# Layer 1 with two single tiles and seven pairs, and differences of weight blocks taken from PSUM while the weights are still being made

## The reference, cut to what matters

```
x: (32, 64, 1024) fp32; condition c[b] in 0..15; two layers, each  x = x + ffn(mix(x))
mix:    m[b] = W_cond[c[b]]^T x[b]           (a 64 x 64 matrix for each of the 32 samples)
layer 0 ffn:  m @ ternary(w0) * column scale + b0            (w0: 1024 x 1024)
layer 1 ffn:  m @ w^T + bias + 4 * (m @ A^T) @ B^T
        w = NF4_LEVELS[q_weight] * q_scale per group of 64   (1024 x 1024), A: 8 x 1024, B: 1024 x 8
```

## Time and profile before

| | us |
|---|---|
| median of 3 runs (lowest, highest) | 360.81 (360.71, 360.83) |
| profiled execution, device time | 360.83 |
| its span | 359.0 |
| TensorE busy | 352.2 (98%) |
| VectorE busy | 242.0 (67%) |
| ScalarE busy | 161.1 (45%) |
| GpSimd busy | 224.7 (63%) |

### The profile page before, as it was taken

One profiled execution on the slowest core, in us unless ns is written; L12 is line 12 of the kernel. 1 busy time (PEld: TensorE's weight loads), 2 busy tenths in 40 slices (PEclk: granted clock), 3 DMA queues, 4 the chain that ended last, 5 costly groups with the idle time before them and its releaser, 6 DMA issues.

```text
span 359.0 us, 5496 instructions
## 1 busy us (share of the span) xinstructions
PE 352.2 (98%) x1832; PEld 298.7 (83%) x1832; DVE 242.0 (67%) x363; ACT 161.1 (45%) x285; POOL 224.7 (63%) x146
## 2 busy tenths in 40 slices
PE   8899999999999999999999999999999999999996
PEld 8768788888888888888888888888888888888884
DVE  5789969896996899873899979355262452634523
ACT  2787467776886877752232314213041130321300
POOL 0488999986976888876520220866366663666632
PEclk9999999999999999999999999999999999999999
DMA  6894411953345245333311330304215032150202
GB/s 235 289 328 138 151 31 30 339 203 115 134 168 181 88 156 203 125 120 121 108 76 62 123 118 3 120 0 155 88 63 181 1 140 103 60 182 2 117 31 88
DMA packets 27838, 44.63 MB, mean 124 GB/s; under 512 B 8834, under 2 KB 17026, under 8 KB 27810
## 3 DMA queue, kind: packets, MB, share of 16 engines
q1 hardware_dynamic: 26242, 43.67, 35.0%
q10 hardware_dynamic: 1568, 0.61, 0.7%
HBM read 27.49 MB, written 16.78 MB: 123 GB/s over the span
## 4 chain that ended last, share of the span: by engine, by line
PE 87%; DVE 3%; POOL 2%; issue 2%; ACT 2%; SPq 1%; DMA 1%; POOLq 0%; DVEq 0%; ACTq 0%
PE acc L1157 33%; PE acc L1195 32%; PE xT L1121 10%; PE acc L1137 6%; PE spare L1121 3%; POOL col_scale L596 2%; PE acc L1222 2%; DMA w_in<-in_L_ffn_w 1%; PE acc L1224 1%; DVE hl L872 1%; PE xT L1204 1%; DVE W L925 1%; ACT hh L684 0%; SPq L428 0%; SPq L426 0%
## 5 line engine op out<-in xcount | busy, mean ns | idle before, releaser
L569 POOL TENSOR_TENSOR X<-X,bias 128x1024 f32<-128x1024 f32 x28 | 67.5, 2412 | 29.3 <-PE xT L1121 29.1
L1157 PE MATMUL acc<-T,hh 128*128 128x512 f32 x192 | 76.0, 396 | 0.0
L1157 PE MATMUL acc<-T,hl 128*128 128x512 f32 x192 | 75.0, 391 | 0.0
L723 ACT ACTIVATE spare<-q_raw 128x512 f32<-128x512 int32 x96 | 56.0, 598 | 19.1 <-DVE side_p L913 5.1
L1195 PE MATMUL acc<-W,hh 128*128 128x512 f32 x192 | 61.1, 389 | 0.0
L1021 DVE TENSOR_TENSOR X<-X,acc 128x512 f32<-128x512 f32 x36 | 24.8, 688 | 34.8 <-PE acc L1195 18.6
L1121 PEld LDWEIGHTS xT<-mix,X 128*128 128x128 f32 x352 | 42.7, 192 | 1.5
L1121 PE MATMUL xT<-mix,X 128*128 128x128 f32 x352 | 42.8, 275 | 0.0
L1195 PEld LDWEIGHTS acc<-W,hh 128*128 128x128 f32 x192 | 36.0, 188 | 7.5
L1157 PEld LDWEIGHTS acc<-T,hl 128*128 128x128 f32 x192 | 36.1, 188 | 7.4
L628 POOL TENSOR_TENSOR X<-X,ys 128x512 f32<-128x512 f32 x18 | 22.6, 1286 | 31.1 <-DVE ys L1010 31.1
(11 more groups left out here) (98 smaller groups left out, 662.0 us busy)
## 6 DMA issues: line engine op xcount, KB each, us to landing
out<-X SPq DMA_DIRECT2D x26, 512.0 KB, 3.0
X<-out SPq DMA_DIRECT2D x16, 512.0 KB, 3.4
X<-in_x SPq DMA_DIRECT2D x12, 512.0 KB, 3.4
q_raw<-in_L_ffn_q_weight SPq DMA_DIRECT2D x16, 256.0 KB, 3.0
w_in<-in_L_ffn_w SPq DMA_DIRECT2D x14, 256.0 KB, 6.5
x_first<-in_x SPq DMA_DIRECT2D x4, 512.0 KB, 4.6
out<-x_first SPq DMA_DIRECT2D x4, 512.0 KB, 6.8
out<-X SPq DMA_DIRECT2D x4, 256.0 KB, 2.0
```

What stands on the lines that cost most here:

```text
L569: pool.tensor_tensor(x_of(g), x_of(g), (bias1 if g >= NT else bias)[:, :], ALU.add).then_inc(s_xb, 1)
L723: act.activation(dst, q_raw[:, d % QS, :, :].rearrange("p o i -> p (o i)"), ACT.Copy, scale=slope, bias=offset).then_inc(s_line, 1)
L1157: mm = pe.matmul(acc[:, bank_of(q), :], a[:, k, :], b, start=(k == 0 and j == 0), stop=(k == KB - 1 and j == len(terms) - 1))
```

## The change

Layer 1 gets two single tiles and seven pairs (`SB = NT + 2`). T1 and T3 are now made during layer 0. ScalarE copies the transposed pieces r = 0 and 1 out of PSUM unrounded (`keep_block`), into the place where the low part of T2 and T3 will be. When the next piece (r = 1 or 2) lies in PSUM, VectorE subtracts the kept one from it (`sum_T13`), ScalarE rounds the difference (`high_T13`) and VectorE writes its low part over it (`low_T13`). T2 and T4 are made in the two single tiles: 24 instructions of VectorE and 8 of ScalarE, dealt out by `SUMS_BY`. `turn_w` of a piece r = 2 or 3 waits for `sum_T13` too. `lines_by` places on ScalarE each line that a maximum of an earlier half tile needs ahead of that half tile's end. The weights lie in SBUF in a new order, so the wait for the spilled first tiles moves from T1's high part to `high_w(4)`. Where low parts were read from, their plain form has the same address (`W01_sums`, `W23_sums`, `W_T4_sums`).

```diff
     WARM = 10
-    SB = NT + 4
...
 
-    W_ORDER = (T1, T2, B11, B21, B22, T3, B12)
-
-
-    NTS = 12
-    COMPLETE = ((T1, 3), (T3, 5), (T2, 6), (T4, 10))
+    W_ORDER = [(B11, 1), (B12, 1), (B21, 1), (B22, 1), (B11, 0), (B12, 0), (B21, 0), (B22, 0),
+               (T1, 0), (T1, 1), (T2, 0), (T2, 1), (T3, 0), (T3, 1)]
+
+
+    NTS = 6
+    SUMS_BY = (0, 8, 15, 21, NTS * HB + 1)
...
 
+    def lines_by(m):
+
+        done = share(2 * NC * ND, m)
+        if done == 0:
+            return 0
+        d, c = divmod(done - 1, 2 * NC)
+        sign, j = divmod(c, NC)
+        return max(share(2 * NL * ND, m), 2 * NL * d + NL * sign + j + 2)
+
     def sums_by(m):
 
-        return NTS * HB * (m - NH * NT) // (NH * (SB - NT))
+        return SUMS_BY[m - NH * NT]
...
 
             if c == T4:
                 return W_T4[:, part, j, :]
-            return (W01, W23)[j // 2][:, W_ORDER.index(c), part, j % 2, :]
...
-            return plain({T1: 1, T3: 3, T2: 4, T4: 5}[c])
+        def as_is(c, j):
+
+
+            if c == T4:
+                return W_T4_sums[:, 1, j, :]
+            return (W01_sums, W23_sums)[j // 2][:, W_ORDER.index((c, j % 2)), 1, :]
...
 
@@ -727,19 +754,33 @@
                 act.wait_ge(s_wT, d + 1)
                 if d == 0:
                     act.wait_ge(s_acc, NH * F)
+                if d == 4:
+                    for t in range(F):
+                        act.wait_ge(s_spill[t], 16)
...
-                            act.activation(w1(0, c, j), t_plain(c), ACT.Copy).then_inc(s_Th, 1)
+            def keep_block(d):
+
+                j, r = divmod(d, 4)
+                act.wait_ge(s_wT, d + 1)
+                act.activation(as_is((T2, T3)[r], j), wT_flat, ACT.Copy).then_inc(s_asis, 1)
+
+            def high_T13(d):
+
+                j, r = divmod(d, 4)
+                c = (T1, T3)[r - 1]
+                act.wait_ge(s_T13, 2 * j + r)
+                act.activation(w1(0, c, j), as_is(c, j), ACT.Copy).then_inc(s_T13h, 1)
+
+            def high_T24(u):
+
+                j, step = divmod(u, NTS)
+                if step == 1:
+                    act.wait_ge(s_T2, 2 * (j + 1))
+                    act.activation(w1(0, T2, j), as_is(T2, j), ACT.Copy).then_inc(s_T2h, 1)
+                elif step == 5:
+                    act.wait_ge(s_T4, 2 * (j + 1))
+                    act.activation(w1(0, T4, j), as_is(T4, j), ACT.Copy).then_inc(s_T4h, 1)
...
@@ -844,16 +884,22 @@
                 for m in (NH * g, NH * g + 1):
                     for d in range(ND):
                         if turned_in(d) == m - 1:
+                            if d % 4 < 2:
+                                keep_block(d)
                             high_w(d)
                     if F <= g < SB - 1 and m % NH == 0:
                         high_x(g + 1, 0)
                         high_x(g + 1, 1)
                     elif m == NH * SB - 2:
                         left_A(0)
+                    for d in range(ND):
+                        if turned_in(d) == m - 1 and d % 4 in (1, 2):
+                            high_T13(d)
                     if g < NT:
-                        lines(share(per, m), share(per, m + 1))
+                        lines(lines_by(m), lines_by(m + 1))
                     else:
-                        high_sums(sums_by(m), sums_by(m + 1))
+                        for u in range(sums_by(m), sums_by(m + 1)):
+                            high_T24(u)
                     if m == NH * F - 2:
                         high_x(F, 0)
...
-                        low_part(T4)
+            def sum_T13(d):
+
+                j, r = divmod(d, 4)
+                dve.wait_ge(s_asis, 2 * (j + 1))
+                dve.tensor_tensor(as_is((T1, T3)[r - 1], j), wT_flat, as_is((T2, T3)[r - 1], j),
+                                  ALU.subtract).then_inc(s_T13, 1)
+
+            def low_T13(d):
+                j, r = divmod(d, 4)
+                c = (T1, T3)[r - 1]
+                dve.wait_ge(s_T13h, 2 * j + r)
+                dve.tensor_tensor(w1(1, c, j), as_is(c, j), w1(0, c, j).bitcast(F32), ALU.subtract
+                                  ).then_inc(s_T13l, 1)
+
+            def low_T4(j):
+                dve.wait_ge(s_T4h, j + 1)
+                dve.tensor_tensor(w1(1, T4, j), as_is(T4, j), w1(0, T4, j).bitcast(F32), ALU.subtract
+                                  ).then_inc(s_T4l, 1)
+
+            def sum_T24(u):
+
+                j, step = divmod(u, NTS)
+                if u == NTS * HB:
+                    low_T4(HB - 1)
+                elif step == 0:
+                    dve.wait_ge(s_T13l, 2 * (j + 1))
+                    dve.tensor_tensor(as_is(T2, j), as_is(T2, j), w1(0, T3, j).bitcast(F32), ALU.add
+                                      ).then_inc(s_T2, 1)
+                elif step == 1:
+                    dve.wait_ge(s_T2, 2 * j + 1)
+                    dve.tensor_tensor(as_is(T2, j), as_is(T2, j), w1(1, T3, j).bitcast(F32), ALU.add
+                                      ).then_inc(s_T2, 1)
+                elif step == 2 and j > 0:
+                    low_T4(j - 1)
+                elif step == 3:
+                    dve.wait_ge(s_T2, 2 * (j + 1))
+                    dve.wait_ge(s_Wl, 4 * (j + 1))
+                    dve.wait_ge(s_acc, NH * NT)
+                    dve.tensor_tensor(as_is(T4, j), w1(0, B21, j).bitcast(F32), as_is(T2, j), ALU.subtract
+                                      ).then_inc(s_T4, 1)
+                elif step == 4:
+                    dve.wait_ge(s_T2h, j + 1)
+                    dve.tensor_tensor(w1(1, T2, j), as_is(T2, j), w1(0, T2, j).bitcast(F32), ALU.subtract
+                                      ).then_inc(s_T2l, 1)
+                elif step == 5:
+                    dve.wait_ge(s_T4, 2 * j + 1)
+                    dve.tensor_tensor(as_is(T4, j), as_is(T4, j), w1(1, B21, j).bitcast(F32), ALU.add
+                                      ).then_inc(s_T4, 1)
...
@@ -1068,16 +1119,22 @@
                     for d in range(ND):
                         if turned_in(d) == m - 1:
                             low_w(d)
+                            if d % 4 in (1, 2):
+                                sum_T13(d)
                     if F <= g < SB - 1 and m % NH == 0:
                         low_x(g + 1, 0)
                         low_x(g + 1, 1)
                     elif m == NH * SB - 2:
                         low_A(0, A12, 1)
                         low_A(0, A11, 0)
+                    for d in range(ND):
+                        if turned_in(d) == m - 1 and d % 4 in (1, 2):
+                            low_T13(d)
                     if g < NT:
                         maxima(share(per, m), share(per, m + 1))
                     else:
-                        sums_of_blocks(sums_by(m), sums_by(m + 1))
+                        for u in range(sums_by(m), sums_by(m + 1)):
+                            sum_T24(u)
...
 
             def right_ready(c):
 
-                if c in (T1, T2, T3, T4):
-                    pe.wait_ge(s_T, NTS * (HB - 1) + {T1: 7, T3: 9, T2: 11, T4: 12}[c])
+                if c in (T1, T3):
+                    pe.wait_ge(s_T13l, 2 * HB)
+                elif c == T2:
+                    pe.wait_ge(s_T2l, HB)
+                elif c == T4:
+                    pe.wait_ge(s_T4l, HB)
...
 
@@ -1218,6 +1279,8 @@
                 pe.wait_ge(s_wn, d + 1)
                 pe.wait_ge(s_ys, NH * F)
                 need(pe, s_Wl, d)
+                if d % 4 in (2, 3):
+                    pe.wait_ge(s_T13, 2 * (d // 4) + d % 4 - 1)
```

More of the change, by code:

```diff
@@ L137, in build @@
     WARM = 10
-    SB = NT + 4
+    SB = NT + 2
     NP = (2 * NT - SB) // 2
@@ L243, in build @@
             T0 = sb("T0", [P, NH, KB, BANK], F32R, first_use)
+        with ExitStack() as second_use:
+            W_T4_sums = sb("W_T4_sums", [P, 2, HB, BANK], F32, second_use)
         W_T4 = sb("W_T4", [P, 2, HB, BANK], F32R)
@@ L249, in build @@
             x_first = sb("x_first", [P, F, T], F32, first_use)
-        W01 = sb("W01", [P, NPR, 2, HB // 2, BANK], F32R)
+        with ExitStack() as second_use:
+            W01_sums = sb("W01_sums", [P, 2 * NPR, 2, BANK], F32, second_use)
+        W01 = sb("W01", [P, 2 * NPR, 2, BANK], F32R)
         with ExitStack() as first_use:
@@ L257, in build @@
             b_wide = sb("b_wide", [P, KB, P], F32, first_use)
-        W23 = sb("W23", [P, NPR, 2, HB // 2, BANK], F32R)
+        with ExitStack() as second_use:
+            W23_sums = sb("W23_sums", [P, 2 * NPR, 2, BANK], F32, second_use)
+        W23 = sb("W23", [P, 2 * NPR, 2, BANK], F32R)
         def w1(part, c, j):
@@ L263, in w1 @@
                 return W_T4[:, part, j, :]
-            return (W01, W23)[j // 2][:, W_ORDER.index(c), part, j % 2, :]
+            return (W01, W23)[j // 2][:, W_ORDER.index((c, j % 2)), part, :]
         def w_raw(k, n):
@@ L380, in build @@
         s_res1 = sem("s_res1")
-        s_T = sem("s_T")
-        s_Th = sem("s_Th")
```

(19 more changed lines are left out.)

## The result

| | before | after |
|---|---|---|
| median of 7 runs (lowest, highest) | 360.71 (360.43, 360.85) | 361.98 (361.82, 362.10) |
| profiled execution | 360.83 | 361.98 |
| its span | 359.0 | 360.1 |

The ratio is 1.0033, 95% interval 1.0023 to 1.0043: slower by 1.3 us. The time lies in the predicted range, 1.1 us above the forecast, above its band of 360.1 to 361.5 and outside of what was called no difference.

What follows compares the result with a forecast made beforehand. TensorE, busy 98% of the span, was taken as the bound. 360.83 less 2.72 for the pair plus 2.85 of TensorE's loss in layer 0 gave 360.96, forecast as 360.9 us; range 358.4 to 363.8.

Steps and rivals of the forecast that it cites:

- band of 360.1 to 361.5: The forecast's own case: TensorE loses 2.0 to 3.4 us in layer 0; chance 0.33.
- the prediction's own signs of being wrong: TensorE's layer 0 waits under 2 or over 3.5 us, low parts often 1.5 us, or a product waiting for a T.
- The pair saves 2.70 to 2.72: Layer 1: two single tiles becoming a pair save TensorE 2.70 us, or 12 matmuls x 0.227 = 2.72.
- Behind odd pieces low part and difference, then a wait for the rounding: VectorE, layer 0, pieces 1, 5, 9: 2.0 us inserted each, with 0.75 us waiting for ScalarE's rounding.
- Waits for GpSimd of six low parts: VectorE, layer 0: low parts wait for GpSimd's current instruction, 2.1 us together, 1.5 of it at the first.
- VectorE's waits for lines are used up: Layer 0: a late VectorE uses its waits for ScalarE's lines in full; with high parts, 7.9 us used.
- Lateness at piece 13: VectorE, layer 0: 11.9 us inserted against 7.9 us of used waits, 4.0 us later at pieces 13 and 14.
- What TensorE loses ahead of piece 14: Layer 0: lateness 4.0 less slack 1.1 gives 2.9 us, partly paid at pieces 4, 6, 8 and 10.
- Layer 1 costs nothing: VectorE's 24 sums in two single tiles end at 195 to 198, before TensorE wants them; no cost.
- VectorE catches up: Rival, layer 0: most lateness falls away, single stalls of 0.3 to 1 us stay, 359.0 us; chance 0.36.
- GpSimd is in the way each time: Rival, layer 0: six low parts wait 6.0 us for GpSimd in place of 2.1, 364.8 us; chance 0.15.
- the new wait: Rival: lines behind a blocked ScalarE, x loads or a late T sum add 1 to 4 us, 362 to 365; chance 0.16.

Runs made afterwards that it cites:

- the first experiment: The changed kernel with four single tiles and six pairs again, keeping the new order of the sums, without the seventh pair: 364.86 us, ratio 1.0110 to the kernel before.
- the second experiment: The changed kernel with each difference's rounding and low part behind the lines and maxima of the same half tile: 359.8 us, ratio 0.9968 to the kernel before.
- The bias experiment: The changed kernel with GpSimd's bias adding in tiles 5 to 15 cut from 1024 columns to 8: 359.9 us, ratio 0.9986 to the kernel before.
- the sixth experiment: The changed kernel with three blocks kept per j, differences taken from SBUF in half tiles 29 to 31, low parts at the end: 363.71 us, ratio 1.0093 to before.

## Why the prediction came out as it did

The mechanism was as predicted, and the sum was too small by 1.1 us. That the time lies in the range says little, since the range took in both signs; the forecast's own band ended 0.5 us below the measured time, the likeliest single outcome was called faster (0.36), and slower had 0.31 together. One of the prediction's own signs of being wrong came, by a little: TensorE's waits in layer 0 are 3.6 us, with 3.5 as the bound. Step by step:

- The pair saves 2.70 to 2.72: 22.64 us for a pair again, and 2.9 by the first experiment. Right.
- Behind odd pieces low part and difference, then a wait for the rounding: 0.70 us each, taken as 0.75. Right: from the low part of the piece to the next maximum the three stretches got 2.0 us longer each (GpSimd's hold left out), as forecast, and the second experiment gave back 2.2 us for the three waits.
- Waits for GpSimd of six low parts, forecast 2.1: they lasted 2.01, 1.14, 0.69, 1.08, 0.69 and 0.82 instead of 0.69, so 2.3. The first was forecast as 1.5 and was 1.3; the even ones, forecast as 0.6 together, had 1.0. The rule of the Trainium skill (SBUF — State Buffer, "SBUF: two separate sides"), that VectorE and GpSimd hold their shared ports for a whole instruction, fits these rows: each of the four held low parts ends 0.54 or 0.55 us after the end of GpSimd's instruction. The bias experiment shows that the hold of 1.3 us at the first one came through to TensorE.
- VectorE's waits for lines are used up: 8.2 to 1.0 us, forecast to fall to under 1. Right; `lines_by` does that, and by itself it makes the kernel before some 0.7 to 0.9 us faster.
- Lateness at piece 13: forecast 4.0, measured 4.9. This is the term that was mis-sized. "The copy of a block stands ahead of the high part of the same piece ... Nothing" was wrong at piece 12: ScalarE was itself late there, its line had waited 0.26 us for GpSimd, and with the copy (0.5 us) in front of the high part `low_w` starts 0.4 us later, 0.34 of it a listed wait. I had looked at the odd pieces of each pair and not at every piece with a copy. The other half of the 0.9 is small: GpSimd's holds 0.2 more, the one late line (0.23 at 134.70, and what hangs on it) 0.1, the waits that could be used up worth 7.3 instead of 7.4 us, and 0.1 of single instructions that start a few hundredths later.
- What TensorE loses ahead of piece 14: forecast 2.9 with 0.5, 0.5, 0.7 and 0.1 at pieces 4, 6, 8 and 10. Measured 3.9, with 1.05, 0.35, 0.52 and 0.25 and the last wait of 1.4 us. Nine tenths of the difference is the lateness above; the other tenth is that TensorE started 0.15 us behind the end of the difference and not 0.05. The 0.2 us that each wait costs beyond its own length I had not in the sum at all; on the way they are absorbed by the same lateness (TensorE starts when VectorE lets it), and only the last one counts. It stands against the 0.3 us by which the stage began earlier.
- Layer 1 costs nothing: VectorE's last T is done at 199.49, which is 195.7 when TensorE's delay of 3.8 at tile 16 (176.62 instead of 172.84) is taken off; forecast 195 to 198. Right. With the low parts at the end it still costs nothing, but there is little room left: in the sixth experiment, where VectorE came into tile 16 some 6 us later, a product waited.

Of the rivals, "VectorE catches up" did not happen, "GpSimd is in the way each time" would have needed 6 us and had 2.3, and the new wait (ScalarE's high part, late behind a line and a copy) exists with 0.34 us. The slower result is the forecast's own case with 1.1 us more, which carried it over the bound of 0.7; on which side of that bound it would fall the sum could not tell.

**The verdict on the change.** Its two ideas pull apart. The seventh pair and the differences from PSUM are worth 2.7 us, `lines_by` some 0.7 to 0.9; the roundings and low parts among the maxima cost more than that, 4.5 us. With the low parts behind the last maximum the same kernel takes 357.5 us, 3.4 less than before and 4.5 less than as it was changed. Putting the high part ahead of the copy on ScalarE, and starting layer 1 with a pair at once, were not tried.

## What to carry to other kernels

Work moved out of an idle stage into a stage whose second engine is at 86% is priced by that engine's lateness at the next place where the bounding engine asks for it: what is inserted, less the waits that can be used, less the slack at that place. Here this sum came within 1 us of 4. Of a step that needs two engines in turn (difference, rounding, low part), put other work of the queue between the turns, or move the tail to where nobody waits. Only the read that frees the bank must be early; rounding and low part need not stand beside it. Work out first whether the place to which the tail moves has the time: it held eight low parts, and not sixteen instructions.

## What the runs showed of the hardware that was not expected

A wait of TensorE costs some 0.2 us more than its own length. In the chain, four 128x128 transposes after a wait have 0.63 us instead of 0.44, at each of the five waits of the changed kernel and at the one of before; the granted clock was 1.0 throughout. The transposes themselves are hardly slower. Without a wait they start 0.23 us behind the start of the matmul before, while it is still in execution, and last 0.60:

```profile
148.30 0.39 PE L1214 MATMUL acc<-T,hl 128*128 128x512 f32 x1
148.53 0.60 PE L1285 MATMUL acc<-ident,side_p 128*128 128x128 f32 x4
```

After a wait this overlap of 0.16 us is gone and they last 0.63 (86.88 above). So a wait shown with 0.3 us costs 0.5.

A chain of VectorE instructions that read SBUF twice takes turns with GpSimd: in the kernel with the low parts at the end, three in a row take 4.71 us while GpSimd's bias instruction beside them is stretched too:

```profile
159.50 2.81 POOL L600 TENSOR_TENSOR X<-X,bias 128x1024 f32<-128x1024 f32 x1
```

2.81 us instead of 2.37. Both lose, by the order of the rows. The first low part (from 158.75) is held by GpSimd's scaling, which ends at 159.54; the bias instruction starts at 159.50 and is lengthened by 0.44, about the time that this low part still takes; and the next one is held until the bias has ended. The bias of 2.85 us at 174.30 had shown the same in the kernel before.
